# First attention of a decoder block on one core: the bias of q and k as one more matmul with a tile of ones, and squares taken straight out of the bank

## The reference

```python
qkv = x @ Wqkv + bqkv
q, k, v = jnp.split(qkv, 3, axis=2)
q = q - q.mean(axis=2, keepdims=True)
k = k - k.mean(axis=2, keepdims=True)
q2 = q * q
k2 = k * k
q2 = q2 / (q2.sum(axis=2, keepdims=True) + EPS_SUM)
q2 = _l2norm(q2, axis=-1)
k2 = k2 / (k2.sum(axis=2, keepdims=True) + EPS_SUM)
k2 = _l2norm(k2, axis=-2)
kv = jnp.einsum('bnc,bnd->bcd', k2, v)
t2 = jnp.einsum('bnc,bcd->bnd', q2, kv) / math.sqrt(N)
return (v + t2) @ Wln + bln
```

## Time and profile before

| | |
|---|---|
| median of 3 runs | 1651.68 us (1650.9 to 1652.71) |
| the profiled execution | 1660.05 us, its span 1658.3 us |
| mean granted TensorE clock | 0.992 of full speed |
| TensorE busy | 1582.1 us (95%) |
| VectorE busy | 1191.1 us (72%) |
| ScalarE busy | 1069.7 us (65%) |
| GpSimd busy | 512.6 us (31%) |
| first matmul of the first attention's projections | 17.20 us |
| last matmul of the first attention | 218.87 us |
| first matmul of the cross attention | 220.93 us |

### The profile page before, as it was taken

One profiled execution on the slowest core, in us unless ns is written; L12 is line 12 of the kernel. 1 busy time (PEld: TensorE's weight loads), 2 busy tenths in 40 slices (PEclk: granted clock), 3 DMA queues, 4 the chain that ended last, 5 costly groups with the idle time before them and its releaser, 6 DMA issues.

```text
span 1658.3 us, 35997 instructions
## 1 busy us (share of the span) xinstructions
PE 1582.1 (95%) x12470; PEld 1337.3 (81%) x12470; DVE 1191.1 (72%) x2765; ACT 1069.7 (65%) x2702; POOL 512.6 (31%) x438
## 2 busy tenths in 40 slices
PE   5999989999999999999999999997999999999997
PEld 4888866777777777777777777776999999999997
DVE  6888947667776767677677777777976666666663
ACT  4545537667666766676676667666876666666664
POOL 3434410000220210300302203104557655554545
PEclk9999989999999999999999999999999999999999
DMA  3121177018095193490660301136778977877773
GB/s 101 39 90 59 46 207 193 1 51 219 22 253 145 64 266 90 137 267 16 184 167 21 114 1 55 40 113 207 165 175 215 224 176 160 184 178 174 169 181 46
DMA packets 164610, 216.14 MB, mean 130 GB/s; under 512 B 16672, under 2 KB 124752, under 8 KB 164432
## 3 DMA queue, kind: packets, MB, share of 16 engines
q1 hardware_dynamic: 134080, 173.77, 36.8%
q0 software_dynamic: 28896, 38.62, 12.7%
q10 hardware_dynamic: 1456, 1.44, 0.3%
HBM read 90.76 MB, written 123.03 MB: 129 GB/s over the span
## 4 chain that ended last, share of the span: by engine, by line
PE 57%; ACT 13%; DVE 8%; issue 4%; DMA 3%; POOL 1%; POOLq 0%; another core or an unknown queue 0%; SPq 0%; DVEq 0%; ACTq 0%
PE ex_H L1814 11%; PE ex_Y L1829 11%; ACT xa_prob L1381 6%; PE xa_work L1221 6%; PE xa_S L1250 5%; PE xa_work L1296 5%; PE xa_work L1279 5%; PE xa_work L1267 5%; PE xa_work L1232 4%; ACT xa_probT L1395 3%; DMA out<-ex_y,ahead_bits 2%; DVE xa_nmax L1507 2%; DVE xa_prob L1519 2%; PE ex_X L1796 2%; PE xa_S L1255 1%
## 5 line engine op out<-in xcount | busy, mean ns | idle before, releaser
L1381 ACT ACTIVATE xa_prob<-xa_S,xa_nmax 128x512 f32<-128x512 f32 (+3 forms) x512 | 266.3, 535 | 117.2 <-DVE xa_nmax L1507 98.1
L1923 POOL DMA_INDIRECT out<-ex_y,ahead_bits x158 | 260.7, 1650 | 215.5 <-ACT ex_y L1862 98.1
L1814 PE MATMUL ex_H<-ex_xT,ex_w 128*128 128x256 f32 x1896 | 246.4, 286 | 6.1 <-DVE ex_xT L1895 3.3
L1814 PEld LDWEIGHTS ex_H<-ex_xT,ex_w 128*128 128x128 f32 x1896 | 231.7, 191 | 7.1 <-issue 7.1
L1829 PE MATMUL ex_Y<-experts_w_hi,ex_hT 128*128 x1264 | 236.6, 280 | 0.0
L1507 DVE TENSOR_REDUCE xa_nmax<-xa_S 128x2 f32<-128x1024 f32 (+3 forms) x256 | 197.7, 813 | 6.6 <-PE xa_S L1255 4.3
L1829 PEld LDWEIGHTS ex_Y<-experts_w_hi,ex_hT 128*128 128x128 f32 x1264 | 198.7, 188 | 0.0
L1692 POOL DMA_INDIRECT expert_rows<-kept_xn,kept_rows x112 | 111.1, 992 | 268.6 <-DVE xa_prob L1519 226.2
L1395 ACT ACTIVATE xa_probT<-xa_work 128x512 f32<-128x512 f32 x256 | 140.0, 603 | 81.8 <-PE xa_work L1267 72.8
L1829 PE MATMUL ex_Y<-experts_w_lo,ex_hT 128*128 x632 | 176.3, 279 | 0.0
L1519 DVE TENSOR_SCALAR xa_prob<-xa_prob,xa_sums 128x512 f32<-128x512 f32 (+3 forms) x512 | 169.2, 383 | 6.8
(11 more groups left out here) (376 smaller groups left out, 3620.9 us busy)
## 6 DMA issues: line engine op xcount, KB each, us to landing
expert_rows<-xa_room_of_w_hi_and SPq DMA_DIRECT2D x256, 273.0 KB
kept_x<-expert_rows SPq DMA_DIRECT2D x52, 273.0 KB
ex_w_raw<-in_w SPq DMA_DIRECT2D x27, 512.0 KB
ahead_ctx<-in_w SPq DMA_DIRECT2D x26, 512.0 KB
ahead_x<-in_w SPq DMA_DIRECT2D x26, 512.0 KB
kept_xn<-expert_rows SPq DMA_DIRECT2D x27, 273.0 KB
experts_w_lo<-in_w SPq DMA_DIRECT2D x6, 1024.0 KB, 5.9
expert_rows<-xa_room_of_w_hi_and SPq DMA_DIRECT2D x32, 136.5 KB
```

Source lines behind the costliest of these rows:

```text
L1381: m = act.activation(prob[n % 2][:, odd, PROB_AT[i]:PROB_AT[i] + width], SB[slot[at]][:, odd, col:col + width], ACT.Exp, bias=nmax[n % 2][ ...
L1814: m = pe.matmul(bank[:, (f % 2) * ROWS:(f % 2 + 1) * ROWS], ww[:, c, f * P:(f + 1) * P], xx[:, c, :], start=(i == 0), stop=(i == len(terms ...
L1923: pool.indirect_dma_start(out, bass.IndirectOffsetOnAxis(tail[j % NT][:, a, 0:1].bitcast(I32), 0), y[j % NY][:, a, :], None, compute_op=AL ...
```

## The change

The bias of q and k no longer is added by VectorE as it copies the bank out. It becomes a seventh matmul of each `qk` tile: the weights are a tile of ones on 64 partitions (`ones_r`, 64 x 128), the moving operand is `bias_qk` (64 x 512), zero but for row 0, the high part of the centred bias, and row 32, its low part. It accumulates into the same bank, and only it ends the accumulation. In the built program this instruction has a tile size of 64 x 128; the other six have 128 x 128. ScalarE then squares k and q straight from the bank, `take_qk` and the SBUF tile `qk` are gone, and a `qk` bank is free when its squares are done (`squared` q) and not when it was copied. The centring of the bias, with the split into the two rows, moves from behind the weights' low parts to the very front of VectorE's program (`center_bias`), ahead of the statistics of the first x. GpSimd gets two more memsets at its start.

```diff
-        qk, vv = cols("qk", 512), cols("vv", 512)
+        vv, bias_qk, ones_r = cols("vv", 512), sb("bias_qk", [HD, 512], F32R), sb("ones_r", [HD, P], F32R)
+        ones_qk = sb("ones_qk", [HD, P])
...
             def turn(key):
                 i = turn_at[key]
-                w.wait_ge(work_ev, turns[i - 4] if i >= 4 else None, i >= 4)
+                before = turns[i - 4] if i >= 4 else None
+                if before is not None and before[0] == "qk":
+                    w.wait_ge(squared, (*before[1:], "q"))
+                elif before is not None:
+                    w.wait_ge(work_ev, before)
                 return bank_of(key)
...
                             m = pe.matmul(bank[:], a[:, c, t * P:(t + 1) * P], ww[:, c, at],
-                                          start=(c == 0 and i == 0), stop=(c == KC - 1 and i == 2))
+                                          start=(c == 0 and i == 0), stop=(kind == "vv" and c == KC - 1 and i == 2))
+                    if kind == "qk":
+                        w.wait_ge(b_mean_of, "ones")
+                        m = pe.matmul(bank[:], ones_r[:], bias_qk[:], start=False, stop=True)
                     m.then_inc(work_pe.of((kind, b, t)), 1)
...
-                    w.wait_ge(work_ev, ("qk", b, t))
-                    act.activation(sq_k[:, t, :], qk[:, t, D:512], ACT.Square, accum_out=s2[b % 2][:, t, 1:2]
+                    w.wait_ge(work_pe, ("qk", b, t))
+                    act.activation(sq_k[:, t, :], bank_of(("qk", b, t))[:, D:512], ACT.Square, accum_out=s2[b % 2][:, t, 1:2]
                                    ).then_inc(squared.of((b, t, "k")), 1)
-                    act.activation(sq_q[b % 2][:, t, :], qk[:, t, 0:D], ACT.Square, accum_out=s2[b % 2][:, t, 0:1]
+                    act.activation(sq_q[b % 2][:, t, :], bank_of(("qk", b, t))[:, 0:D], ACT.Square, accum_out=s2[b % 2][:, t, 0:1]
...
-            def take_qk(b, t):
-                w.wait_ge(b_mean_of, "centered")
-                w.wait_ge(squared, (b - 1, t, "q4") if b >= 1 else None, b >= 1)
-                w.wait_ge(work_pe, ("qk", b, t))
-                dve.tensor_tensor(qk[:, t, :], bank_of(("qk", b, t))[:], bias[:, 0:512], op=add
-                                  ).then_inc(work_ev.of(("qk", b, t)), 1)
...
+            def center_bias():
+                hi_row, lo_row = slice(0, 1), slice(HD // 2, HD // 2 + 1)
...
+                w.wait_ge(b_mean_of, "centered")
+                w.wait_ge(ones_set, "ones_qk")
+                dve.tensor_copy(bias_qk[hi_row, :], bias[hi_row, 0:512]).then_inc(b_mean_of.of("hi"), 1)
+                dve.tensor_copy(bias_qk[lo_row, :], bias[lo_row, 0:512]).then_inc(b_mean_of.of("again"), 1)
+                w.wait_ge(b_mean_of, "again")
+                dve.tensor_tensor(bias_qk[lo_row, :], bias[lo_row, 0:512], f32(bias_qk[lo_row, :]), op=sub
+                                  ).then_inc(b_mean_of.of("lo"), 1)
+                dve.tensor_copy(ones_r[:], ones_qk[:]).then_inc(b_mean_of.of("ones"), 1)
+
+            center_bias()
             find_mean(0)
```

More of the change, by code:

```diff
@@ L333, in first_attention @@
         const = signal("const", ["zero", "ident"])
-        ones_set = signal("ones_set", ["power", "ones", "half"])
+        ones_set = signal("ones_set", ["zeros_qk", "ones_qk", "power", "ones", "half"])
         wqkv_in, wln_in, wvT_in = (landed(n, ["in"]) for n in ("wqkv_in", "wln_in", "wvT_in"))
         bqkv_in, bvT_in, bln_in = (landed(n, ["in"]) for n in ("bqkv_in", "bvT_in", "bln_in"))
-        w_mean_of, b_mean_of = signal("w_mean_of", ["sum", "neg"]), signal("b_mean_of", ["sum", "neg", "centered"])
+        w_mean_of, b_mean_of = signal("w_mean_of", ["sum", "neg"]), signal("b_mean_of", ["sum", "neg", "centered", "hi", "again", "lo", "ones"])
         w_hi, w_lo = signal("w_hi", ["qkv", "wln", "wvT", "bvB"]), signal("w_lo", ["qkv", "wln", "wvT", "bvB"])
@@ L344, in first_attention @@
         xT_pe, xT_hi, xT_lo = (signal(n, in_blocks) for n in ("xT_pe", "xT_hi", "xT_lo"))
-        work_pe, work_ev = signal("work_pe", turns), signal("work_ev", turns)
+        work_pe, work_ev = signal("work_pe", turns), signal("work_ev", [key for key in turns if key[0] != "qk"])
         v_hi, v_lo, xb_ev = (signal(n, halves) for n in ("v_hi", "v_lo", "xb_ev"))
@@ L739, in repeat_halves @@
                 dve.tensor_scalar(ahead.bqT[:], ahead.bqT[:], HD ** -0.5, None, mult).then_inc(bq_scaled.of(0), 1)
+            def center_bias():
+                hi_row, lo_row = slice(0, 1), slice(HD // 2, HD // 2 + 1)
+                w.wait_ge(bqkv_in, "in")
+                dve.tensor_reduce(b_mean[:], bias[:, 0:512].rearrange("p (j n) -> p j n", j=2), AX.X, add
+                                  ).then_inc(b_mean_of.of("sum"), 1)
+                w.wait_ge(b_mean_of, "sum")
+                dve.tensor_scalar(b_mean[:], b_mean[:], -1.0 / D, None, mult).then_inc(b_mean_of.of("neg"), 1)
+                w.wait_ge(b_mean_of, "neg")
+                for j in range(2):
+                    i = dve.tensor_scalar(bias[:, j * D:(j + 1) * D], bias[:, j * D:(j + 1) * D], b_mean[:, j:j + 1], None, add)
+                i.then_inc(b_mean_of.of("centered"), 1)
+                w.wait_ge(b_mean_of, "centered")
[7 more added lines that the diff above has]
+            center_bias()
             find_mean(0)
@@ L763, in vector @@
             dve.tensor_tensor(bvB[1], over_columns(bvT[:], P), f32(bvB[0]), op=sub).then_inc(w_lo.of("bvB"), 1)
[L764 to L772, removed]
             find_mean(1)
@@ L776, in vector @@
                 if b < B:
-                    for t in range(2):
-                        take_qk(b, t)
                     if b == 0:
@@ L818, in vector @@
                                       ).then_inc(kn_max.of(done), 1)
-                if b < B:
-                    take_qk(b, 2)
-                    take_qk(b, 3)
                 if done >= 0:
@@ L864, in gpsimd @@
                                pattern=[[-1, P]], channel_multiplier=1).then_inc(const.of("ident"), 1)
+            pool.memset(f32(bias_qk[:]), 0.0).then_inc(ones_set.of("zeros_qk"), 1)
+            pool.memset(ones_qk[:], 1.0).then_inc(ones_set.of("ones_qk"), 1)
             pool.memset(power[:], -0.5).then_inc(ones_set.of("power"), 1)
```

## The result

| | before | after |
|---|---|---|
| median of 10 runs each, us | 1651.18 | 1661.09 |
| ratio, 95% interval | | 1.0054, 1.0035 to 1.0072 |
| measured again on another chip | 1659.58 (20 runs) | 1668.89 (7 runs) |
| its ratio, 95% interval | | 1.0047, 1.0025 to 1.0069 |
| last stretch of the first attention begins (two profiles of before, three of after) | 199.93, 200.37 | 206.47, 206.99, 206.35 |

The account below looks back on a forecast made before the run. TensorE, busy for 95% of the span, bounds the kernel, with waits on a VectorE loop in long batches. Start 1.2, first batch 2.2, second 1.0 and six batches 4.9 sum to +9.3 us: 1661.0 us, range 1654 to 1665.

Parts of the forecast that it names:

- Price of the added matmul: TensorE, q and k projections: each lone 64-row matmul costs 0.62 us, its 0.23 stream plus switching tile shape both ways.
- Start: VectorE's front: bias centring delays the first statistics, so everything behind starts 1.2 us late (0.4 to 2.0).
- First batch: First attention's first batch: four new matmuls cost 2.9 us, less 0.7 regained at its end: +2.2 us.
- The 0.7 us at the batch's end: First batch's end: TensorE waits less for ScalarE, whose squares no longer await copies; gain 0 to 1.7, taken as 0.7.
- Second batch: First attention, 36.29 to 58.52 us: TensorE's 20.86 busy plus 2.5 for new matmuls makes 23.3, +1.0 us.
- Six batches: First attention from 58.52 us: TensorE needs 24.4 us in each, 146.3 against 141.4: +4.9 us.
- Last stretch: End of the first attention, without projections: no change, 0 us.
- Removing the copies gives 0.5 us: VectorE's loop behind the norm: the fourth small step still waits for GpSimd's port, so 0.5 us shorter, not 2.6.
- line 711 ending before 127.5: VectorE's fourth small step behind the norm: ending that early in a chunk batch would make the forecast wrong.
- stream only: Rival, chance 0.16: each added matmul costs TensorE only 0.23 us, no switch; whole +0.3 us, 1652.0.
- faster: Rival, chance 0.05: 0.23 us matmuls and small steps ahead of GpSimd, loop 2.6 us shorter; whole -3.5 us, 1648.2.
- The clock: Rival, chance 0.07: emptied TensorE lets the granted clock fall once per batch, seven times; +12.6 us on top, 1673.

Follow-up runs that it names:

- paired: Kernel after, with the bias matmuls of two neighbouring tiles side by side, so half the switches of tile shape: 1653.02 us in one run.
- rows128: Kernel after, with biases and ones on all 128 partitions (zeros in the new bias rows): 1650.88 us against 1650.48 for the kernel before, ratio 0.9993.
- casts_act: Kernel after, with the casts of biases and ones on ScalarE and the subtraction behind the first normalisation: 1676.5 us in one run.
- before_again: The kernel before, unchanged, profiled once more: 1648.82 us in one run.
- no_bias: Kernel after without any bias matmul, the bias of q and k left out; copies stay gone: 1645.72 us in one run.
- matmul_only: Kernel before plus a 64-row matmul of zeros in each projection tile of q and k; copies stay: 1669.66 us in one run.
- weigh_early: Kernel before, with the scaling of the finished batch's queries moved on VectorE from behind the norm to ahead of the means: 1661.07 against 1661.84 us, ratio 0.9992.

## Why the prediction was right, step by step

The direction and its cause are right: the price of the added matmuls, most of it the switches, makes TensorE set each of the six batches. That the total comes within 0.1 us (1661.0 predicted, 1661.09 measured) is luck; the interval of the measured difference alone is 6 us wide. Of its terms the price and the start are right, the second batch (by 1.8 us) and the six (by 1.2) are too high. Up to the last stretch the profiles show 6.5 us in the mean where the sum has 9.3. The last stretch, put at nothing, adds about 1.7 in the mean; the 1 to 2 us that are left to the measured 9.3 and 9.9 lie behind the first attention, where no profile can place them. One argument was wrong.

- *Price of the added matmul, 0.62 us*: measured 0.63 in after; 0.40 of it goes with a switch pair (paired), and all but 0.23 with the shape (rows128). The first one, where the matmuls around it are 0.43 us apart, costs 1.02 where 1.0 was taken (20.61 to 22.49 in after, less two pitches of 0.43). Right, and it decided. The Trainium skill's rule that a change of tiling mode drains TensorE (TensorEngine Tiling (Array Packing), "Key Properties") agrees with these rows, 0.40 us for a change and back; the other one, that a single matmul of small contraction takes as long as a full one (TensorE: Matmul & The Clock Gate, "Why this matters for your kernels"), holds for its stream alone: the second of a pair adds 0.86 - 0.63 = 0.23.
- *Start, +1.2*: 17.20 to 18.34, +1.14 (+1.0 in the mean of the profiles). Right, and by the stated work: casts_act takes it back. The casts took 0.42 each where 0.5 was taken.
- *First batch, +2.2*: 19.09 to 21.59 us, +2.5 in that pair of profiles, but 1.3 to 3.0 over the pairs of all of them (19.1 and 19.6 before; 20.9, 21.6 and 22.1 after). The first projections run at pitches of 0.43 us and later ones at 0.23, and the profiles differ in where that ends: at 20.3 us in before, 22.2 in before_again. The 0.7 us at the batch's end came back (the wait of the earlier trace rows is 1.68 now). The stated reason suffices: in no_bias, without the copies and without the added matmul, it is 1.68, and ScalarE there waits for the transposes, the bound that the prediction named. It is 1.68 in matmul_only too, where the squares still wait for the copies and TensorE is later. So either half of the change gives it, and after has both.
- *Second batch, +1.0*: measured -0.8, and -0.1 against before_again. The mis-sized term. It took the 20.86 us of busy time at a clock of 0.92 as TensorE's need and added 2.5. With the clock at 1.00 the batch takes 21.47 in before_again and 21.4 in all profiles of after: the new matmuls fall into the waits of a batch that TensorE did not fill. In rows128 it takes 19.81, TensorE busy throughout, and 19.81 + 4 x 0.40 = 21.4. About nothing was the right term.
- *Six batches, +4.9*: measured +3.7 (145.1 less 141.4). TensorE alone sets them, as forecast, and no wait at the norm is left, but at 24.2 and not at 24.4. The addition of 21.9 + 2.5 took a busy time with the restarts after waits in it; no_bias's batch without waits is 21.63, and 21.63 + 4 x 0.63 = 24.15.
- *Last stretch, 0*: not so in the mean. It took 21.0 and 18.6 in before, 20.2, 21.3 and 22.9 in after. All ten profiles of kernels with the added matmul or the freed VectorE have a low-clock part there, but of the three of before and weigh_early two have none. The one steady difference that the rows show ahead of it is that TensorE, which idles there for ScalarE's part of k squared, does so for 2.07 us and not 1.72. Whether that or chance lets the clock fall was not tried. Those two profiles have their low-clock part just behind: before_again from 220.4 to 222.4 us (0.50), weigh_early from 218.0 to 220.0 (0.50). So part of this term is which side of the border the fall lies on. With it the cross attention begins 8.1 us later on the mean of the profiles, against 9.3 predicted.
- *Removing the copies gives 0.5 us, since the fourth small step is blocked by GpSimd*: wrong. Line 711 ran at 129.79 for 0.16, inside the record of GpSimd's line 910; that one, on 2 columns, held nobody up, and all four were through before line 916. From norm to line 523 the forecast had 4.9 us; no_bias has 3.8. The sentence "line 711 ending before 127.5" as a sign against the forecast came true, counted from the norm: line 711 ends 0.7 us behind its end, where 127.5 would be 1.2. It didn't hurt the number, because 24.1 and 21.9 lay both under what TensorE needs. The loop's true gain was neither figure: 1.2 us (no_bias), because its other arm, from y through the load of x and the statistics to the norm, got no shorter (19.2 to 19.6 us).
- *The rivals*: stream only and faster both fell with the price; with the price removed (rows128) the batches come near the first's 22.8, and the whole ends at before, where the first had it. The clock did not fall once per batch: it is 1.00 in all six.

## What to carry to other kernels

Before a small helper matmul is put into a dense stream, compare its tile's rows with its neighbours': padding the operands with zeros to the same shape cost 0.23 us here, the smaller shape 0.63. Price work taken off an engine by the engine that is next: 4.3 us less of VectorE in a batch (22.24 in matmul_only, 17.93 in after) gave 0.3 us, since TensorE stood right behind it. And when a term starts from a busy time, take it from a stretch without waits and at full clock.

## What the runs showed of the hardware

- A lone 64 by 128 tile of 512 columns between 128 by 128 ones costs 0.63 us, a pair of them 0.86, the same with 128 rows 0.23 each. The pitches are 0.33 in, 0.42 over and 0.34 after; across a switch a weight load starts together with its matmul, not one matmul ahead.
- GpSimd's powers of 2 columns (0.70 us of record) and of 4 (1.01) did not hold up a VectorE step of two SBUF operands, 0.16 us inside the record of each; its subtraction of 1024 columns held one for 2.06. The Trainium skill's exclusive lock "for the whole instruction" (SBUF — State Buffer, "SBUF: two separate sides") fits the second and not the first. Whether the small ones take no lock or only hold it for a part of their record is not shown; starts and ends on GpSimd are rough in the profile.
- ScalarE squares 256 columns out of a bank in 0.36 to 0.37 us and out of SBUF in 0.40 to 0.42.
- The last stretch takes 18.6 us at a granted clock of 1.00, 20.2 at a mean of 0.92, 21.0 at 0.84 and 22.9 at 0.78. Within one kernel that makes 2.4 us (before) and 2.7 (after), the largest variation seen ahead of the cross attention and over a quarter of the change.
